# Layer-program kernel on one core: weights of the fold in double banks and another order, first latent keys roped there, the start's loads and the latent stage's reciprocals taken another way

## The reference, cut to what matters

```python
x = x + _L0_xattn_ref(_layernorm(x), ctx_512, ...)   # 16 heads of 16, causal, 32 keys of the context
x = x + _L0_attn_ref(_layernorm(x), ...)             # 16 heads of 128, one shared key
x = x + _L0_ffn_ref(_layernorm(x), ...)              # 16 blocks of 64, 4 chosen
x = x + _L1_xattn_ref(_layernorm(x), ctx_512, ...)   # latent attention, 257 keys, rope
x = x + _L1_attn_ref(_layernorm(x), ...)             # 16 heads of 16, causal
x = x + _L1_ffn_ref(_layernorm(x), ...)              # 8 experts of width 512, one chosen
```

```python
q_hk = (hidden_q @ Wq.T).reshape(b, s, H, K)
q_big = jnp.einsum('bshk,hkq->bshq', q_hk, w_kc_q)
kv_rope = kv_c * cos[None] + _rotate_half(kv_c) * sin[None]
q_r = jnp.einsum('bshq,hqr->bhsr', q_big, W_qr)
k_r = jnp.einsum('bld,hdr->bhlr', kv_rope, W_kr)
scores = jnp.einsum('bhsr,bhlr->bhsl', q_r, k_r)
attn = jax.nn.softmax(scores, axis=-1)
ctx_c = jnp.einsum('bhsl,bld->bhsd', attn, kv_rope)
ctx_lat = jnp.einsum('bhsd,hkd->bshk', ctx_c, w_kc_kv)
out = ctx_lat.reshape(b, s, H * K) @ Wo.T
```

## Time and profile before

| | us |
|---|---|
| median of 3 runs | 1452.88 |
| lowest, highest | 1446.67, 1453.36 |
| the profiled execution | 1452.64 |
| its span, first to last instruction | 1450.8 |
| PE busy | 1241.3 (86%) |
| DVE, ACT, POOL busy | 802.4, 510.3, 289.4 |

### The profile page before, as it was taken

The page is one execution under the profiler, slowest core; times in us unless marked ns, Lnnn a source line. Parts: engine busy times, 40 slices in busy tenths (PEclk is TensorE's granted clock), DMA queues, the critical chain, the costliest instruction groups (busy, mean ns, idle before and its releaser), DMA issues. The chain is left out here.

```text
span 1450.8 us, 33350 instructions
## 1 busy us (share of the span) xinstructions
PE 1241.3 (86%) x12959; PEld 962.9 (66%) x12960; DVE 802.4 (55%) x1940; ACT 510.3 (35%) x1471; POOL 289.4 (20%) x347
## 2 busy tenths in 40 slices
PE   0899979999999976999957999999986999709998
PEld 0677757777777756888746766666655888605665
DVE  4467755655556535555215777777773999322222
ACT  0345533322233211211005555555551666202221
POOL 2100003221122200000014454444510000041222
PEclk9999989999999988999758999999998999559999
DMA  9000000000000007400010000000034200112221
GB/s 304 0 1 0 0 1 1 1 0 0 0 0 0 0 1 194 110 0 0 1 34 12 11 17 15 15 7 14 16 118 165 69 0 0 58 65 39 41 38 20
DMA packets 45232, 49.62 MB, mean 34 GB/s; under 512 B 11568, under 2 KB 37296, under 8 KB 44592
## 3 DMA queue, kind: packets, MB, share of 16 engines
q1 hardware_dynamic: 41088, 44.49, 10.5%
q0 software_dynamic: 4080, 4.22, 1.4%
HBM read 39.33 MB, written 10.28 MB: 34 GB/s over the span
## 5 line engine op out<-in xcount | busy, mean ns | idle before, releaser
L703 POOL TENSOR_TENSOR attn_qT_squared<-attn_qT 128x512 f32<-128x512 f32 x64 | 67.0, 1047 | 402.0 <-ACT attn_qT L646 402.0
L1383 ACT ACTIVATE xattn_exps<-xattn_ps_s,xattn_top 128x256 f32<-128x256 f32 x256 | 118.0, 479 | 61.9 <-DVE xattn_top L1461 61.9
L553 PEld LDWEIGHTS attn_ps_q<-attn_xnT,w_b_q 128*128 128x128 f32 x1024 | 120.0, 194 | 23.2 <-issue 12.6
L553 PE MATMUL attn_ps_q<-attn_xnT,w_b_q 128*128 128x128 f32 x1024 | 126.9, 281 | 0.0
L605 PE MATMUL attn_ps_out<-w_b_o,attn_oT 128*128 128x256 f32 x512 | 117.3, 389 | 8.7 <-ACT attn_oT L665 5.2
L605 PEld LDWEIGHTS attn_ps_out<-w_b_o,attn_oT 128*128 128x128 f32 x512 | 98.7, 195 | 24.0 <-issue 6.0
L1458 DVE TENSOR_REDUCE xattn_raw_top<-xattn_ps_s 128x4 f32<-128x1024 f32 x64 | 77.8, 1216 | 57.1 <-PE xattn_ps_s L1281 57.1
L646 ACT COPY attn_qT<-attn_ps_q 128x512 f32<-128x512 f32 x64 | 37.2, 581 | 164.8 <-PE attn_ps_q L553 164.8
L1468 DVE STREAM_TRANSPOSE xattn_expsT<-xattn_exps 128x1024 f32<-128x1024 f32 x64 | 79.5, 1241 | 17.5 <-ACT xattn_exps L1383 17.5
L1259 PE MATMUL xattn_ps_o<-xattn_xnT,all_d_a 128*128 128x128 f32 x512 | 67.3, 287 | 8.9 <-ACT xattn_inverse L1413 8.9
L1259 PEld LDWEIGHTS xattn_ps_o<-xattn_xnT,all_d_a 128*128 128x128 f32 x512 | 61.9, 198 | 18.3 <-issue 9.8
(11 more groups left out here) (281 smaller groups left out, 2524.7 us busy)
## 6 DMA issues: line engine op xcount, KB each, us to landing
xattn_kv_raw<-in_ctx SPq DMA_DIRECT2D x64, 64.0 KB, 1.8
moe_gate<-in_f_gate SPq DMA_DIRECT2D x8, 512.0 KB, 7.3
moe_up<-in_f_up SPq DMA_DIRECT2D x8, 512.0 KB, 7.2
moe_down<-in_f_down SPq DMA_DIRECT2D x8, 512.0 KB, 9.3
sorted_x<-all_zeros SPq DMA_DIRECT2D x1, 2944.0 KB, 13.8
experts_x_in<-sorted_x SPq DMA_DIRECT2D x23, 128.0 KB, 2.3
all_x<-in_x SPq DMA_DIRECT2D x4, 512.0 KB, 7.4
w_b_q<-in_b_wq SPq DMA_DIRECT2D x1, 2048.0 KB, 13.9
```

Of the source, the lines that this page charges most:

```text
L553: last = nc.tensor.matmul(ps_q[g % 2][:, h * P:(h + 1) * P], wq[:, c, head * DH:(head + 1) * DH], xnT[u][:, c, :], start=(c == 0), stop=(c ...
L703: nc.gpsimd.tensor_tensor(qT_squared[:, :, g, :], qT[:, :, g, :], qT[:, :, g, :], ALU.mult)\
L1383: nc.scalar.activation(exps[g % 2][:, nkeys * k:nkeys * (k + 1)], ps_s[g % 2][:, nkeys * k:nkeys * (k + 1)], ACT.Exp, bias=top[u][:, n:n + ...
```

## The change

1. *Loads.* The first part of x goes ahead of consts, the weights b and c are issued in the next stage, and statistics come before the tables. The scaling of b_q is cut to pieces of 256 columns. In `small_attention` DVE waits only for consts and the tables, not for the weights.
2. *Fold.* Two sets of banks and of r1, r2; PE's order is new.
3. *Rope.* A class `RopedKeys` keeps the tables and keys in the SBUF of the ffn weights c. SP loads tables and the keys of tiles 0 and 1 in the fold stage, POOL multiplies and joins tile 0 there.
4. *Latent stage.* `spread_inverse`, its ACT copies and DVE's 0/1 matrix are gone. SP stores the rows of reciprocals to DRAM (4x512), waits for that, and loads them back onto 128 partitions in two DMAs of 256 KB. `keys` and `queries` wait for one weighed sum each. PSUM banks change places. The gates are issued after the last reciprocals. ACT runs one Exp ahead.

The diff, cut to its core:

```diff
@@ fold_weights, SP and POOL
+            pool.wait_ge(early.s["tables_in"], 16 * 2 * TB)
+            early.multiply(pool, 0, 0, None)
+            early.join(pool, 0)
...
+            early.load_tables(sp, tables_d)
+            for t in range(2):
+                early.load_keys(sp, ctx_d, t, t)
             sp.wait_ge(s["last_ready"], 2)
@@ fold_weights, PE
+            for g in range(2):
+                out_weights(g, 0)
+                first_products(g, range(0, half // 2))
+                out_weights(g, 1)
+                first_products(g, range(half // 2, half)).then_inc(s["r1_made"], 1)
+            second_products(0)
+            for n in range(2):
+                out_weights(2, n)
+            second_products(1)
+            third_products(0)
+            for n in range(2):
+                out_weights(3, n)
+            third_products(1)
@@ latent_attention, SP
+            def inverse_of(t, u):
+                sp.wait_ge(s["tail_ready"], t + 1)
+                sp.dma_start(inverse_d, tailT[1:P:SEQ, :, :]).then_inc(s["inverse_stored"], 16)
+                sp.wait_ge(s["inverse_stored"], 16 * t + 16)
+                for odd in range(2):
+                    sp.dma_start(inverse[64 * odd:64 * odd + 64, :, :],
+                                 inverse_d[:, odd, :].unsqueeze(0).to_broadcast([64, TB, DIM])).then_inc(s[f"inverse_in{u}"], 16)
+
             def step(t, u, live):
-                raw(t, u)
+                if live(0) and live(-2):
+                    raw(t, u)
+                if live(-2):
+                    inverse_of(t - 2, u)
...
+                if live(0):
+                    last(t, u)
@@ latent_attention, POOL
-                pool.wait_ge(s["inverse_out"], 2 * t + 2)
+                pool.wait_ge(s[f"inverse_in{u}"], 16 * t + 32 - 16 * u)
@@ latent_attention, PE: keys, queries, step
+                wait_count(pe, s["sum_ready"], TB * (t - 2) + 1 + part)
...
-                    wait_count(pe, s["inverse_out"], 2 * (t - 1))
+                wait_count(pe, s["sum_ready"], TB * (t - 2) + 3 + part)
...
-                if live(-1):
-                    pe.wait_ge(s["sum_ready"], TB * t)
                 if live(1):
                     keys(t + 1, 0)
-                if live(-1):
-                    if isinstance(t, int) and t == 1:
-                        pe.wait_ge(s["spread_made"], 1)
-                    spread_inverse(1 - u)
@@ latent_attention, ACT
+            nc.scalar.activation(tried[:, :], ident[:, 0:1], ACT.Exp)
...
-                if live(-1):
-                    inverse_out(t - 1)
@@ program, loads
+                load_x(0)
                 sp.dma_start(consts[:, :], d["consts"]).then_inc(got_consts, 16)
-                for n in range(0, TILES, x_part):
-                    sp.dma_start(x_sb[:, n:n + x_part, :], chunks(d["x"])[:, n:n + x_part, :]).then_inc(got_x[n // x_part], 16)
+                load_x(x_part)
...
+                load_x(2 * x_part)
+                load_x(3 * x_part)
                 sp.dma_start(a_o[:, :, :], chunks(d["a_wo"])).then_inc(got_a, 16)
-                sp.dma_start(b_q[:, :, :], chunks(d["b_wq"])).then_inc(got_b, 16)
...
+        def load_bc(sp):
+            sp.dma_start(b_g[:, :], d["b_g"]).then_inc(got_b, 16)
+            sp.dma_start(b_q[:, :, :], chunks(d["b_wq"])).then_inc(got_b, 16)
...
@@ program, scale_b
-                nc.gpsimd.tensor_scalar(b_q[:, c, :], b_q[:, c, :], b_g[:, c:c + 1], None, ALU.mult).then_inc(b_scaled, 1)
+                for n in range(0, HEADS * DH, SCALED):
+                    nc.gpsimd.tensor_scalar(b_q[:, c, n:n + SCALED], b_q[:, c, n:n + SCALED], b_g[:, c:c + 1], None, ALU.mult)\
+                      .then_inc(b_scaled, 1)
```

265 lines of the change are left out of this document (131 added, 134 removed).

## The result

| | us |
|---|---|
| before, median of 4 runs | 1452.02 (1446.67 to 1453.36) |
| after, median of 4 runs | 1393.38 (1389.77 to 1395.96) |
| ratio | 0.9601, 95% interval 0.9567 to 0.9635 |
| profiled execution of after | 1394.44, its span 1392.4 |

Executions more than 1.5% above the fastest of their kernel (one of dense_even, two of best_even, three of best_warm) are left out of every ratio and range of this text.

A forecast was written before the change was run, and what follows sets the result against it. PE was taken as the bound nearly everywhere (86% of the span); 1452.6 - 14.3 + 1 - 7 - 13 - 30 - 1.5 = 1387.8, forecast 1388 us, range 1370 to 1410.

The forecast's parts named there:

- Latent steps: 14 latent steps: spread products and PE's waits for reciprocals and copies leave PE's row, 2.15 us a step, -30 us.
- finish without a wait: Sign in the latent steps: finish on PE does not wait for POOL, with a step of 18.3 us.
- Rival 2: Latent steps: the way through DRAM is late, 14 us per microsecond beyond 7.4 from tailT to landing; 1403, chance 0.15.
- First keys: Behind the fold: PE's 12.72 us wait for the first roped keys goes, -13.0 us.
- Start: Start of the kernel: PE begins at 20.4 instead of 34.70 us, -14.3 us.
- POOL's pieces: First attention: POOL's 18 scaling pieces run beside its steps and can hold DVE, +1 us (0 to +6).
- Rival 4: First attention: the clock rises soon, after 6 us instead of 46; 1371, chance 0.08.
- Fold: Fold stage: the clock falls later, 10 to 20 us after the start; 34.2 instead of 40.9 us, -7.
- rival 3: Fold: its start meets half clock and keeps it, +6 instead of -7; 1401, chance 0.07.
- With 15 at full: Step of the fold's sum: 15 us at full clock, the 10.3 left take 19.2, 34.2 in all.
- Rival 1: Fold: the clock holds throughout, 25.3 us at full clock, -15.6 instead of -7; 1379, chance 0.15.
- End of the stage: Last two tiles of the latent stage: nothing hides the reciprocals' way, -1.5 us (-3 to +4).

The follow-up runs named there:

- dense_even: Kernel after with the fold's dense products set singly, one after every six thin ones; ratio to before 0.9542, three executions from 1382.75 to 1392.56 us.
- best_even: Kernel after with x issued ahead of weights a, reciprocal rows read in 4 KB runs, single dense products after six thin ones; ratio to before 0.9547.
- best_warm: best_even plus 13 unread products on PE in the first stage, before x is there; ratio 0.9535, three executions from 1380.90 to 1384.18 us.
- two_stores: Kernel after with the reciprocals' store to DRAM and its wait made twice per tile before the loads; 1433.32 us.
- start_back: Kernel after with the loads, DVE's tables and POOL's scaling of b where they were before; 1407.81 us, ratio to before 0.9694.
- x_first: Kernel after with all four parts of x issued ahead of the a weights and the context's weights on SP; 1392.24 us.
- spread_back: Kernel after with the latent reciprocals spread as before by PE products and ACT copies, nothing through DRAM; 1422.41 us, ratio to before 0.9797.

## Why the prediction was right or wrong

**Latent steps**, -30: right in size and in what leaves PE's row (-32.1, and -30.3 by the middle one, 256.5, of the seven kernels with these steps). What was wrong inside: that the reciprocals' way fits "by 2 us". The term that was mis-sized is the landing of the two loads, taken as 3.8 us, of which 1.0 for the 450 KB beyond the row had no row behind it; 5.2 pass from their issue to POOL. So "finish without a wait" did not come; POOL began 10.8 us behind scores 0, not 9.4. It cost 5.5 us, and 4.4 that the sum didn't have were won at the keys' and queries' products. Rival 2 had the right resource, but put the edge at 7.4 us from tailT to landing, and finish is tied to the way in steps where it takes 6.7; two_stores shows that each microsecond more is paid in full, and more.

**First keys**, -13.0: right, -12.9.

**Start**, -14.3: -11.7. Right that DVE's roots move from SP's end to x's landing and that POOL is no longer beside them. Mis-sized was "x at about 14 us and its last statistics at 15.5": x was in at 15.2, and 2.88 us of statistics for two parts came behind, to 18.1. The 4.4 us from the first root instruction to PE were 4.5 (18.47 to 23.01).

**POOL's pieces**, +1 (0 to +6): 0, by start_back.

**First attention**: no term of the change, yet -7.2. Rival 4 named it, but not by its mechanism. The clock rose 29.5 us in, not 6, and the lengths are 165 to 172 in kernels with the same code and start. One trace does not give the length of a stretch in which the clock changes, and I had taken before's 46 us as its property.

**Fold**, -7: it was +4.8, which is rival 3 (+6), given 0.07. The step that failed is "With 15 at full": it was 1.9 in this execution, 10.6 in five others, where the sum gives 10.6 + (25.3 - 10.6) x 1.86 = 37.9, with 3.3 to the first turn 41.2, and 41.7 was measured. The costs of the products were right; the moment of the fall was a guess, and the order's true effect is a choice between -2.7 and +4.8. Rival 1, the clock held with this order, came in none of the seven traces of it. The Trainium skill (TensorE: Matmul & The Clock Gate, Part 1) has the clock go down with idleness; here it went down in x_first after PE had been busy 10.64 of 10.65 us, stayed down in after with 43.99 of 44.10, and stayed up in dense_even with 31.58 of 31.70, so busy time by itself does not tell. The page's remark that the ramp differs from run to run of one kernel agrees with the first attention.

**End of the stage**, -1.5: +3.75. The way through DRAM costs 1.5 more than spread_back's (43.5 for 42.0), where nothing hides it. The other 2.3, by which spread_back is longer than before with the same work, are the clock's: the stretch has 0.91 in before and 0.84 in spread_back and in after, and PE is busy 26.4 us with the records that took 24.1. First before, then spread_back:

```profile
1071.76:1111.50 39.74, 24.14 (x489) 16.69 (x473) 21.82 (x65) 9.78 (x37) 5.50 (x8) 0.91 0.13 45
1037.05:1079.04 41.99, 26.40 (x488) 18.24 (x473) 21.80 (x65) 9.79 (x37) 5.51 (x8) 0.84 0.11 37
```

**attn, ffn**, -1.6 and -2.0: their code is the same, and the other kernels have 493 to 495 for both together, as before had; only after and two_stores have 490.5. It is the clock again: PE is busy 446.0 us there with the records that took 449.7 in before.

## What to carry to other kernels

A value that must reach all partitions can go through DRAM at the cost of one engine's queue instead of products, copies and banks. Count the whole way from the issue of the store to the reader, with the landing of a load of that size, and look what is late next: here there was nothing to spare, though PE's waits were small, and an extra 1.7 us on the way cost 2.45 a step. Where the clock changes inside a stage, compare several executions by stage before crediting an edit with the difference, and where products of few columns stand in long rows, try wide ones singly between them and look at the clock: single ones after six kept it up here in three of three traces, a pair after twelve didn't in the one that was taken.
